# Query tokens in a fused ViT tower: five split float32r products per tile against two plain float32 products

## The chip, the cores and the metric

The kernel runs on one core of a Trainium2 chip. A time is the device time of one execution in microseconds (us), and the metric is the median over several executions. TensorE is called PE below, VectorE DVE, ScalarE ACT, GpSimd POOL and the DMA-issuing SyncE SP.

## What is computed

From images x (128 images, 12 channels, 224 x 224, float32), each 16 x 16 patch is summed per channel, which gives 196 tokens of 12 numbers, and each token is multiplied by a 12 x 192 matrix. Of the 196 tokens of an image the first 64 are queries and the other 132 are keys. After a layer norm the queries attend to the keys; the attention output goes through a projection, and the sum is `h`. Then comes the part that this change touches:

```
x2 = layernorm(h)                          # 192 channels
scores = sigmoid(x2 @ gate_weight.T)       # 8 experts; the best 2 are chosen through 4 groups
h1 = einsum('td,eid->tei', x2, w1)         # 8 experts, 128 inner channels
h3 = einsum('td,eid->tei', x2, w3)
y  = einsum('tei,edi,te->td', silu(h1) * h3, w2, cw)
z  = silu(x2 @ sw1.T) * (x2 @ sw3.T) @ sw2.T   # a shared ninth expert
out = h + y + z
```

All inputs and the output are float32. "First layer" means the products with w1, w3, sw1 and sw3; "router" means the product with gate_weight.

## The kernel before, in words

The 128 images are worked through in 8 groups of 16. A group has 2112 key tokens and 1024 query tokens, cut into 7 chunks: five of keys (384 to 512 tokens) and two of queries (512 each). For each chunk 9 experts are run, so a group has 63 steps: steps 0 to 44 are the key steps and steps 45 to 62 the query steps. PE's program is written out by hand (`ffn_pe`, L1527). In each step it issues the w1 product of the next step (`layer1`, k = 0), the w3 product of this step (k = 1), the second layer of the step two back (`layer2`, L1509), and then the items that a plan gives to this step (`AQ_PLAN`, `AK_PLAN`, L79 to L140): attention, transposes, router, sums. ACT makes silu of h1 (L913), POOL multiplies it with the routing weight that an SP-issued DMA has spread over the partitions (L752, L561), DVE multiplies that with h3 (L1266), and PE's second layer reads it. While one group runs, DVE and ACT sum the image tiles of later groups (L960, L801), and in the query steps DVE also computes the next group's key routing (`gates`, L1157).

A matmul contracts over partitions, of which there are 128, and there are 192 channels. For keys, the normalized token depends on 12 pooled numbers and a constant, so their first layer is one bf16 product of 126 rows (L1524). Queries have no such short form. Their normalized 192 channels are transposed in two parts, channels 0 to 127 and 128 to 191, by the item `XT` (L1451): four rounds a group, in steps 21, 22, 26 and 27. In an even round, four transposes fill a PSUM bank of 512 columns. In an odd round each tile's last 64 channels are written twice, by a transpose to partitions 0 to 63 and by a product with the identity to partitions 64 to 127 (L1460, L1461). ACT then copies the bank as float32r (L859) into `x0h` or `x1h`, the high part. DVE waits for that copy (`high_ready`) and subtracts it from the bank (L1152), which gives the low part `x0l` or `x1l`. The weights are split in the same way once, at the start (L1013 to L1019): `WT0h`, `WT0l`, and `WT1s`, which holds the high part of the last 64 channels in its first 64 partitions and the low part in the other 64. The router's weights `gT0h`, `gT0l`, `gT1s` likewise. With these, `layer1` makes a query product of 512 tokens as five float32r products (`products`, L1350 to L1354), added up in one PSUM bank: high x high, low weight x high, high weight x low for the 128 channels, then stacked weights x high and stacked weights x low for the 64. The router item `GQ` (L1462, step 28, two a group) does the same with 8 output rows.

The start of the kernel runs a list of rounds (`PREP`, L418) on PE with copies by DVE or ACT: transposing the weights (`W0`, `W1`), the router's (`gate`), and `Wc` (L1325), which multiplies the weights by the 12-row token matrix for the keys, in plain float32 and in three products: high, low and stacked. Between the rounds, DVE, ACT and POOL sum the first group's 21 image tiles. Only three tile buffers exist, so a tile's DMA waits until all of these engines have read the one three back.

Of the kernel before, what the change touches and what calls it, by code (L numbers as in the profile page):

```python
# [26 lines left out]
F32R = mybir.dt.float32r  # L27
# [115 lines left out]
DVE_KINDS = ("tok", "S", "H", "AH", "XT")  # L143
# [124 lines left out]
def build(nc, x, cw, proj_w, proj_b, gate_w, gate_b, w1, w2, w3, sw1, sw2, sw3, out):  # L268
    ctx = ExitStack()
    with ctx:  # L270
# [22 lines left out]
        WT0h = sb("WT0h", [128, 2 * EX * INTER], F32R)  # L293
        WT0l = sb("WT0l", [128, 2 * EX * INTER], F32R)
        WT1s = sb("WT1s", [128, 2 * EX * INTER], F32R)
        Wx = sb("Wx", [SPL * SPL * UC, 2 * EX * INTER + NE], BF16)
        W2T = sb("W2T", [INTER, EX, D])
        gT0h, gT0l, gT1s = sb("gT0h", [128, NE], F32R), sb("gT0l", [128, NE], F32R), sb("gT1s", [128, NE], F32R)
# [7 lines left out]
        x0h, x0l = sb("x0h", [128, 1024], F32R), sb("x0l", [128, 1024], F32R)  # L306
        x1h, x1l = sb("x1h", [128, 1024], F32R), sb("x1l", [128, 1024], F32R)
# [87 lines left out]
        high_ready = sem("high_ready")  # L395
# [63 lines left out]
        def split_dst(r):  # L459

            kind, i = PREP[r]
            if kind == "gate":
                return NE, (gT0h if i == 0 else gT1s)[:, :], gT0l[:, :] if i == 0 else None
            a, k = w4(i)
            a, n = a * 128, k * 128
            return n, (WT0h if kind == "W0" else WT1s)[:, a:a + n], WT0l[:, a:a + n] if kind == "W0" else None
# [312 lines left out]
        def _(act):  # L779
# [39 lines left out]
            def item(g, kind, i):  # L819
# [4 lines left out]
                if kind not in PE_KINDS or kind in DVE_KINDS and kind != "XT":  # L824
                    return
# [17 lines left out]
                elif kind == "X":  # L843
                    b0, nb = S_IMGS[i]
                    keys_out(X2T, ps[0:126, 0:nb * NK].rearrange("p (b t) -> p b t", b=nb), b0, nb).then_inc(aux_act, 1)
                elif kind == "ET":
                    if i == 0:

                        wait(act, cw_out[0], g.at(16, 16))
                        wait(act, cw_out[1], g.at(64, 64))  # L850
                    nc.scalar.copy(ET[:, 8 * (i % 2):8 * (i % 2) + 8, :].rearrange("p u q -> p (u q)"), ps[0:HT, :])\
                      .then_inc(aux_act, 1)
                elif kind == "M":
                    half, part = divmod(i, 2)
                    n = 2 * D if part == 0 else D
                    nc.scalar.copy(Msb[0:8 * CH, half, 2 * D * part:2 * D * part + n], ps[0:8 * CH, 0:n]).then_inc(aux_act, 1)
                elif kind == "XT":
                    q, part = divmod(i, 2)
                    nc.scalar.copy((x0h if part == 0 else x1h)[:, 512 * q:512 * q + 512], ps[:, :]).then_inc(high_ready, 1)  # L859
                elif kind == "GQ":  # L860
                    nc.scalar.copy(logT[:, 512 * i:512 * i + 512], ps[0:NE, :]).then_inc(aux_act, 1)
                elif kind in ("G", "GK"):
                    a, b = (0, 8) if kind == "G" else (8, GT)
                    nc.scalar.activation(gt[:, 0, NE * a:NE * b], ps[:, 0:NE * (b - a)], ACT.Exp, scale=-1.0)\
                      .then_inc(aux_act, 1)
                elif kind in ("CK", "CQ"):
                    n = 64 if (kind, i) == ("CK", 4) else 512
                    st = cw_stage[(kind, i)][:, 0:n]
                    nc.scalar.copy(st, ps[0:NE, 0:n]).then_inc(aux_act, 1)
                    at = 512 * i + (1024 if kind == "CK" else 0)  # L870
                    act.wait_ge(aux_act, g.at(BYACT[-1], BYACT[r]))
                    act.dma_start(cw_rows[g.par, :, at:at + n], st)\
                       .then_inc(cw_out[2 if kind == "CQ" else min(i, 1)], 16)
# [67 lines left out]
        def _(dve):  # L941
# [60 lines left out]
            def prep(r):  # L1002
# [10 lines left out]
                elif PREP[r][0] in ("W0", "W1", "gate"):  # L1013
                    n, high, low = split_dst(r)
                    ps = aux[r % 2]
                    plink(v.tensor_copy(high, ps[:, 0:n]))
                    if low is None:
                        high, low, ps = high[64:128], high[64:128], ps[64:128]
                    v.tensor_tensor(out=low, in0=ps[:, 0:n], in1=high.bitcast(F32), op=ALU.subtract).then_inc(prep_dve, 1)  # L1019
# [47 lines left out]
            def item(g, kind, i):  # L1067
# [80 lines left out]
                elif kind == "XT":  # L1148
                    q, part = divmod(i, 2)
                    high, low = (x0h, x0l) if part == 0 else (x1h, x1l)  # L1150
                    dve.wait_ge(high_ready, g.at(4, i + 1))
                    v.tensor_tensor(out=low[:, 512 * q:512 * q + 512], in0=ps[:, :],  # L1152
                                    in1=high[:, 512 * q:512 * q + 512].bitcast(F32), op=ALU.subtract).then_inc(aux_dve, 1)
                elif kind in ("gate_k", "gate_q"):
                    gates(g, i, *((8, GT, ("GK", 0)) if kind == "gate_k" else (0, 8, ("G", 0))))
# [128 lines left out]
        def _(pe):  # L1284
# [3 lines left out]
            for r, (kind, i) in enumerate(PREP):  # L1288
# [19 lines left out]
                elif kind == "gate":  # L1308
# [3 lines left out]
                    if i == 1:  # L1312
                        last = mm(ps[64:128, 0:NE], g_nat[:, 128:D], ident[0:NE, 0:NE], start=True, stop=True)
# [4 lines left out]
                elif kind == "W1":  # L1318

                    a, k = w4(i)  # L1320
                    for j in range(k):
                        nc.tensor.transpose(ps[0:64, 128 * j:128 * j + 128], w13_nat[:, a + j, 128:D], ident[:, :])
                        last = mm(ps[64:128, 128 * j:128 * j + 128], w13_nat[:, a + j, 128:D], ident[:, :],
                                  start=True, stop=True)
                elif kind == "Wc":  # L1325
# [3 lines left out]
                    for lo, hi, parts in ((0, m, [w[:, a:a + m] for w in (WT0h, WT0l, WT1s)]),  # L1329
                                          (m, n, [w[:, :] for w in (gT0h, gT0l, gT1s)])):  # L1330
                        if lo < hi:
                            for q in range(3):
                                last = mm(ps[0:CH, lo:hi], CWcT[q // 2], parts[q].bitcast(F32), start=(q == 0), stop=(q == 2))
# [15 lines left out]

            def products(o, left, right):  # L1350

                for q in range(len(left)):
                    ins = mm(o, left[q], right[q], start=(q == 0), stop=(q == len(left) - 1))  # L1353
                return ins  # L1354

            def item(g, kind, i):
# [94 lines left out]
                elif kind == "XT":  # L1451
# [3 lines left out]
                    for j in range(4):  # L1455
# [3 lines left out]
                        else:  # L1459
                            nc.tensor.transpose(ps[0:64, at], x2q[:, j, 128:D], ident[:, :])  # L1460
                            last = mm(ps[64:128, at], x2q[:, j, 128:D], ident[:, :], start=True, stop=True)  # L1461
                elif kind == "GQ":  # L1462

                    at = slice(512 * i, 512 * i + 512)
                    last = products(ps[0:NE, :], [gT0h[:, :], gT0l[:, :], gT0h[:, :], gT1s[:, :], gT1s[:, :]],
                                    [x0h[:, at], x0h[:, at], x0l[:, at], x1h[:, at], x1l[:, at]])
# [46 lines left out]
            def layer1(g, step, k):  # L1513
# [5 lines left out]
                if query:  # L1519
                    w, at = slice(w, w + INTER), slice(col, col + n)  # L1520
                    last = products(o[:, 0:n], [WT0h[:, w], WT0l[:, w], WT0h[:, w], WT1s[:, w], WT1s[:, w]],
                                    [x0h[:, at], x0h[:, at], x0l[:, at], x1h[:, at], x1l[:, at]])
# [60 lines left out]
```

## Time and profile before

| what | value |
|---|---|
| median of 3 runs | 1799.77 us (1799.73 to 1805.82) |
| the profiled execution's own time | 1794.41 us |
| its span, first to last instruction | 1792.6 us |
| mean granted TensorE clock | 0.950 of full speed |
| PE matmul busy | 84% of the span |
| DVE, ACT, POOL busy | 66%, 49%, 42% |
| HBM traffic | 242 GB/s over the span |

The profile records one execution. Its own time is 1.8 us above its span, and 5.4 us below the median of the runs. Busy time of PE is a union of matmuls whose ends are modelled, so the distance from one matmul's start to the next one's is the better measure of what a matmul costs while PE never waits.

### The profile page before, as it was taken

Reading aid. Unit: us, or ns where it says so; the run is one execution under the profiler, and the core shown is the slowest. Engines: PE = TensorE matmul, PEld = TensorE weight load, DVE = VectorE, ACT = ScalarE, POOL = GpSimd, SP = SyncE. Lnnn points to the kernel's source line nnn. Section 1 sums busy time; section 2 is a strip of 40 time slices with the busy share of each in tenths; the row PEclk is TensorE's granted clock in tenths of the full one; section 3 lists DMA queues with packets and bytes.
Section 4 is the critical chain, followed back from the end, with each engine's and each line's share of the span. In section 5 each row is a group of like instructions: output and inputs, shape, how many; then the busy total and the mean of one; then the engine's idle time right before and its main releaser. Section 6 shows DMA issues by size and latency. Waiting matters only on the chain. (4 is left out here: it accounts for less than half of the span.)

```text
span 1792.6 us, 29976 instructions
## 1 busy us (share of the span) xinstructions
PE 1509.6 (84%) x9094; PEld 1184.0 (66%) x9094; DVE 1178.3 (66%) x2060; ACT 879.1 (49%) x2809; POOL 761.5 (42%) x761
## 2 busy tenths in 40 slices
PE   1721698999899988989899988999899988999997
PEld 1201575877668765877668765777668765887686
DVE  5856686687768666667768676677768666355511
ACT  2333655556545645547535655546545644335310
POOL 4327244633373234623464243633373233733431
PEclk9955799999999989999999999999999989999998
DMA  9897777778677777777777687768777775223320
GB/s 341 358 361 276 300 276 272 276 276 291 245 280 260 281 262 268 273 275 274 256 247 297 241 292 278 276 253 299 256 263 280 268 262 158 70 64 111 96 84 24
DMA packets 127672, 440.11 MB, mean 246 GB/s; under 512 B 14221, under 2 KB 80930, under 8 KB 105998
## 3 DMA queue, kind: packets, MB, share of 16 engines
q1 hardware_dynamic: 126390, 436.79, 67.6%
q10 hardware_dynamic: 1112, 1.30, 0.3%
q8 instruction: 76, 1.25, 0.3%
q14 instruction: 94, 0.77, 0.1%
HBM read 413.86 MB, written 20.07 MB: 242 GB/s over the span
## 5 line engine op out<-in xcount | busy, mean ns | idle before, releaser
L752 POOL TENSOR_TENSOR ffn<-ffn 128x384 f32<-128x384 f32 (+2 forms) x448 | 510.3, 1144 | 888.7 <-ACT ffn L913 810.2
L1509 PE MATMUL bank<-W2T,ffn 128*128 128x192 f32 (+1 forms) x3600 | 705.7, 333 | 10.2 <-ACT stage L890 5.0
L1509 PEld LDWEIGHTS bank<-W2T,ffn 128*128 128x128 f32 (+1 forms) x3600 | 604.9, 191 | 79.8 <-issue 16.5
L1266 DVE TENSOR_TENSOR ffn<-bank,ffn 128x384 f32<-128x384 f32 (+2 forms) x504 | 310.4, 617 | 349.3 <-PE bank L1353 151.8
L960 DVE TENSOR_REDUCE pooled<-xt 128x3 f32<-128x768 f32 (+2 forms) x375 | 447.8, 1195 | 18.5 <-DMA xt<-in_x 17.9
L913 ACT ACTIVATE ffn<-bank 128x384 f32<-128x384 f32 (+2 forms) x504 | 272.3, 542 | 370.3 <-PE bank L1524 141.3
L801 ACT ACTIVATE xt<-xt 128x256 f32<-128x256 f32 x809 | 329.7, 414 | 83.7 <-DMA xt<-in_x 76.1
L1524 PE MATMUL bank<-X2T,Wx 126*128 126x384 bf16 (+2 forms) x720 | 202.6, 355 | 46.7 <-DVE ffn L1266 31.9
L801 ACT ACTIVATION_READ_ACCUMULATOR xt<-xt 128x1 f32 x809 | 158.6, 196 | 0.0
L1353 PE MATMUL bank<-x0h,WT0h 128*128 128x512 f32 x288 | 130.5, 453 | 6.0 <-DVE ffn L1266 6.0
L1524 PEld LDWEIGHTS bank<-X2T,Wx 126*128 126x128 bf16 x720 | 58.2, 100 | 103.7 <-DVE ffn L1266 46.1
L1353 PE MATMUL bank<-x1l,WT1s 128*128 128x512 f32 x288 | 113.9, 395 | 0.0
L1353 PE MATMUL bank<-x1h,WT1s 128*128 128x512 f32 x288 | 113.8, 395 | 0.0
L1353 PE MATMUL bank<-x0l,WT0h 128*128 128x512 f32 x288 | 113.6, 395 | 0.0
L1353 PE MATMUL bank<-x0h,WT0l 128*128 128x512 f32 x288 | 113.6, 394 | 0.0
L707 POOL TENSOR_TENSOR stat<-stat,mhalf 98x16 f32<-98x16 f32 x32 | 94.8, 2970 | 21.9 <-DVE stat L1085 13.6
L1353 PEld LDWEIGHTS bank<-x0h,WT0h 128*128 128x128 f32 x288 | 54.3, 189 | 24.6 <-DVE ffn L1266 9.0
L1353 PEld LDWEIGHTS bank<-x1l,WT1s 128*128 128x128 f32 x288 | 54.0, 188 | 13.1
L1353 PEld LDWEIGHTS bank<-x0l,WT0h 128*128 128x128 f32 x288 | 54.0, 188 | 13.0
L1353 PEld LDWEIGHTS bank<-x1h,WT1s 128*128 128x128 f32 x288 | 54.0, 188 | 13.0
L1353 PEld LDWEIGHTS bank<-x0h,WT0l 128*128 128x128 f32 x288 | 54.4, 189 | 5.9
L841 ACT CAST UTq<-bank 126x128 bf16<-126x128 f32 x64 | 17.0, 265 | 84.0 <-PE bank L1433 84.0
(234 smaller groups left out, 1786.1 us busy)
## 6 DMA issues: line engine op xcount, KB each, us to landing
xt<-in_x SPq DMA_DIRECT2D x168, 1792.0 KB, 8.2
ffn<-cw_rows SPq DMA_DIRECT2D x192, 256.0 KB, 6.8
ffn<-cw_rows SPq DMA_DIRECT2D x192, 192.0 KB, 8.8
out<-stage SPq DMA_DIRECT2D x192, 96.0 KB
ffn<-cw_rows SPq DMA_DIRECT2D x64, 224.0 KB, 7.1
h2q<-Msb SPq DMA_DIRECT2D x64, 54.0 KB
ffn<-in_L_ffn_w SPq DMA_DIRECT2D x2, 768.0 KB
attw<-in_L_ffn_w SPq DMA_DIRECT2D x1, 512.0 KB
```

Source lines behind the costliest of these rows:

```text
L707: nc.gpsimd.tensor_tensor(out=stat[:, 3 * a + 1, u], in0=stat[:, 3 * a, u], in1=mhalf[0:HT, u], op=ALU.pow).then_inc(rstd_ready, 1)
L752: nc.gpsimd.tensor_tensor(out=cwb[slot][:, 0:n], in0=silu[(g.par + step) % 2][:, 0:n], in1=cwb[slot][:, 0:n], op=ALU.mult).then_inc(scaled, 1)
L801: last = nc.scalar.activation(src[:, :, j, :], src[:, :, j, :], ACT.Copy, accum_out=pooled[:, t // HALF, at:at + 1])
L841: nc.scalar.copy(UTq[:, :].rearrange("p (b t) -> p b t", b=GB)[:, 2 * i:2 * i + 2, :], src[:, :, 0:NQ])
L913: nc.scalar.activation(silu[(g.par + step) % 2][:, 0:n], h_ps(g, step, 0)[:, 0:n], ACT.Silu)\
L960: ins = v.tensor_reduce(out=pooled[:, t // HALF, at + lo:at + hi], in_=src[:, lo:hi, :, :], axis=AX.XY, op=ALU.add)
L1266: v.tensor_tensor(out=h[step % HR][:, 0:n], in0=h_ps(g, step, 1)[:, 0:n], in1=(silu[p] if e == NE else cwb[(c * NE + e) % CW_RING])[:, 0:n ...
L1353: ins = mm(o, left[q], right[q], start=(q == 0), stop=(q == len(left) - 1))
L1509: last = mm(o, h[step % HR][:, 128 * t:128 * t + m], W2T[:, e, :], start=(e == 0 and t % 2 == 0), stop=(e == NE), skip_group_check=True)
L1524: last = mm(o[:, 0:n], Wx[:, w:w + INTER], X2T[:, col:col + n], start=True, stop=True)
```

## The change

The float32r type is gone, and with it all low parts. `x0` and `x1` hold the transposed tokens in float32 (128 and 64 partitions), `WT0` and `WT1` the first-layer weights, `gT0` and `gT1` the router's. Each query product is made of two float32 products, one over 128 rows and one over 64. `XT` becomes a round that ACT alone empties: it leaves the list of DVE's kinds and no longer has the second write of the 64 channels. In the start, a weight round is one DVE copy, without a subtraction, `W1` has one transpose a tile, and `Wc` has two products in place of three. The semaphore `high_ready` is gone.

```diff
-DVE_KINDS = ("tok", "S", "H", "AH", "XT")
+DVE_KINDS = ("tok", "S", "H", "AH")
...
-        WT0h = sb("WT0h", [128, 2 * EX * INTER], F32R)
-        WT0l = sb("WT0l", [128, 2 * EX * INTER], F32R)
-        WT1s = sb("WT1s", [128, 2 * EX * INTER], F32R)
+        WT0, WT1 = sb("WT0", [128, 2 * EX * INTER]), sb("WT1", [D - 128, 2 * EX * INTER])
...
-        x0h, x0l = sb("x0h", [128, 1024], F32R), sb("x0l", [128, 1024], F32R)
-        x1h, x1l = sb("x1h", [128, 1024], F32R), sb("x1l", [128, 1024], F32R)
+        x0, x1 = sb("x0", [128, 1024]), sb("x1", [D - 128, 1024])
...
                 elif kind == "XT":
                     q, part = divmod(i, 2)
-                    nc.scalar.copy((x0h if part == 0 else x1h)[:, 512 * q:512 * q + 512], ps[:, :]).then_inc(high_ready, 1)
+                    x, n = (x0, 128) if part == 0 else (x1, D - 128)
+                    nc.scalar.copy(x[:, 512 * q:512 * q + 512], ps[0:n, :]).then_inc(aux_act, 1)
...
                 elif PREP[r][0] in ("W0", "W1", "gate"):
-                    n, high, low = split_dst(r)
-                    ps = aux[r % 2]
-                    plink(v.tensor_copy(high, ps[:, 0:n]))
-                    if low is None:
-                        high, low, ps = high[64:128], high[64:128], ps[64:128]
-                    v.tensor_tensor(out=low, in0=ps[:, 0:n], in1=high.bitcast(F32), op=ALU.subtract).then_inc(prep_dve, 1)
+                    v.tensor_copy(*transposed(r)).then_inc(prep_dve, 1)
...
-                elif kind == "XT":
-                    q, part = divmod(i, 2)
-                    high, low = (x0h, x0l) if part == 0 else (x1h, x1l)
-                    dve.wait_ge(high_ready, g.at(4, i + 1))
-                    v.tensor_tensor(out=low[:, 512 * q:512 * q + 512], in0=ps[:, :],
-                                    in1=high[:, 512 * q:512 * q + 512].bitcast(F32), op=ALU.subtract).then_inc(aux_dve, 1)
...
                         else:
-                            nc.tensor.transpose(ps[0:64, at], x2q[:, j, 128:D], ident[:, :])
-                            last = mm(ps[64:128, at], x2q[:, j, 128:D], ident[:, :], start=True, stop=True)
+                            last = nc.tensor.transpose(ps[0:64, at], x2q[:, j, 128:D], ident[:, :])
                 elif kind == "GQ":
 
                     at = slice(512 * i, 512 * i + 512)
-                    last = products(ps[0:NE, :], [gT0h[:, :], gT0l[:, :], gT0h[:, :], gT1s[:, :], gT1s[:, :]],
-                                    [x0h[:, at], x0h[:, at], x0l[:, at], x1h[:, at], x1l[:, at]])
+                    mm(ps[0:NE, :], gT0[:, :], x0[:, at], start=True, stop=False)
+                    last = mm(ps[0:NE, :], gT1[:, :], x1[:, at], start=False, stop=True)
...
                 if query:
                     w, at = slice(w, w + INTER), slice(col, col + n)
-                    last = products(o[:, 0:n], [WT0h[:, w], WT0l[:, w], WT0h[:, w], WT1s[:, w], WT1s[:, w]],
-                                    [x0h[:, at], x0h[:, at], x0l[:, at], x1h[:, at], x1l[:, at]])
+                    mm(o[:, 0:n], WT0[:, w], x0[:, at], start=True, stop=False)
+                    last = mm(o[:, 0:n], WT1[:, w], x1[:, at], start=False, stop=True)
```

## Rows read from the trace of the kernel before

**Rows 1.** The page: busy time of each engine over the span.

```profile
PE 1509.6 (84%) x9094; PEld 1184.0 (66%) x9094; DVE 1178.3 (66%) x2060; ACT 879.1 (49%) x2809; POOL 761.5 (42%) x761
```

**Rows 2.** Windows by stage: stretch, length, busy of each engine, PEclk, DMA share, GB/s.

```profile
320.00:391.60 71.60, 69.95 (x400) 59.12 (x399) 51.65 (x73) 39.76 (x147) 34.49 (x30) 1.00 0.69 254
391.60:517.90 126.30, 109.95 (x722) 84.43 (x722) 91.18 (x180) 70.54 (x211) 52.41 (x45) 0.99 0.80 288
...
589.40:722.90 133.50, 114.11 (x723) 87.51 (x722) 91.08 (x181) 70.75 (x211) 52.55 (x45) 0.95 0.77 273
...
1711.50:1777.20 65.70, 65.70 (x325) 55.92 (x324) 13.35 (x20) 11.07 (x20) 20.22 (x16) 1.00 0.16 48
```

**Rows 3.** Timeline of PE, one query step: start, us, operation, shapes, count.

```profile
354.67 0.53 PE L1353 MATMUL bank<-x0h,WT0h 128*128 128x512 f32 x1
355.03 0.39 PE L1353 MATMUL bank<-x0h,WT0l 128*128 128x512 f32 x1
...
357.13 1.46 PE L1509 MATMUL bank<-W2T,ffn 128*128 128x192 f32 x8
358.30 0.53 PE L1353 MATMUL bank<-x0h,WT0h 128*128 128x512 f32 x1
```

**Rows 4.** Timeline of PE in the start, plain float32 products of `Wc`.

```profile
67.43 1.02 PE L1333 MATMUL bank<-WT0h,rq 128*12 128x512 f32 x2
...
74.30 1.02 PE L1333 MATMUL bank<-WT1s,gs 128*12 128x512 f32 x2
```

**Rows 5.** Groups of PE instructions, shapes apart: busy, mean ns | idle before.

```profile
L1509 PE MATMUL bank<-W2T,ffn 128*128 128x192 f32 x3456 | 671.7, 332 | 10.2 <-ACT stage L890 5.0 <-DVE stage L1247 4.4
L1353 PE MATMUL bank<-x0h,WT0h 128*128 128x512 f32 x288 | 130.5, 453 | 6.0 <-DVE ffn L1266 6.0
L1458 PE MATMUL bank<-ident,attw 128*128 128x128 f32 x64 | 10.0, 279 | 16.6 <-DVE attw L1146 9.3 <-issue 7.3
```

**Rows 6.** The same view of weight loads.

```profile
L1509 PEld LDWEIGHTS bank<-W2T,ffn 128*128 128x128 f32 x3456 | 590.9, 193 | 65.4 <-ACT stage L890 13.3 <-DVE stage L1247 7.0 <-issue 2.1
```

**Rows 7.** Timeline of PE around steps 21 and 22, the first two `XT` rounds.

```profile
451.56 0.63 PE L1458 MATMUL bank<-ident,attw 128*128 128x128 f32 x4 [1.09 <-DVE attw L1146]
452.02 0.25 PE L1449 MATMUL bank<-CWx,UTq 126*128 126x192 bf16 x1
...
454.19 0.27 PE L1460 MATMUL bank<-ident,attw 128*64 128x128 f32 x1
454.39 0.43 PE L1461 MATMUL bank<-ident,attw 128*64 128x128 f32 x2
...
456.54 0.26 PE L1449 MATMUL bank<-CWx,UTq 126*128 126x192 bf16 x1
```

**Rows 8.** Who uses `x1l` (ns min/median/max, first and last start), and DVE's wait there.

```profile
L1152 DVE TENSOR_TENSOR x1l<-bank,x1h x16: 691/692/692, 259.4 to 1675.0; 128x512 fp32r<-128x512 f32 x16
...
ACT x1h L859: 34.0, 16
```

**Rows 9.** The longest of PE's waits in 320 to 391.6: total, times, longest.

```profile
PE bank L1353 <- DVE ffn L1266: 0.8, 1, 0.8
```

**Rows 10.** Timelines of PE and POOL at the start of the next group.

```profile
397.88 0.68 PE L1402 MATMUL bank<-ident,attw 64*128 64x64 f32 x8 [1.87 <-DVE attw L1105]
...
394.77 2.91 POOL L752 TENSOR_TENSOR ffn<-ffn 128x384 f32<-128x384 f32 x3 [8.40 <-DMA ffn<-cw_rows]
```

**Rows 11.** Groups of DVE instructions in 0 to 192: busy, mean ns | idle before.

```profile
L1019 DVE TENSOR_TENSOR WT0l<-bank,WT0h 128x512 fp32r<-128x512 f32 x4 | 2.8, 692 | 0.1
```

**Rows 12.** Windows of the start, columns as in rows 2.

```profile
60.00:72.00 12.00, 10.93 (x24) 2.65 (x24) 8.84 (x15) 5.20 (x24) 4.62 (x10) 1.00 1.01 430
72.00:80.00 8.00, 4.36 (x13) 1.03 (x12) 7.75 (x10) 2.66 (x12) 3.40 (x7) 1.00 0.51 183
```

**Rows 13.** Timeline of PE, a product with 64 rows and the one after.

```profile
424.15 0.56 PE L1426 MATMUL bank<-projT,Asb 64*96 64x192 f32 x2
424.64 0.50 PE L1524 MATMUL bank<-X2T,Wx 126*128 126x384 bf16 x2
```

More of the change, by code:

```diff
@@ L26 @@
 BF16 = mybir.dt.bfloat16
-F32R = mybir.dt.float32r
 ACT = mybir.ActivationFunctionType
@@ L291, in build @@
         projT = sb("projT", [NQ, 3, D])
-        WT0h = sb("WT0h", [128, 2 * EX * INTER], F32R)
-        WT0l = sb("WT0l", [128, 2 * EX * INTER], F32R)
-        WT1s = sb("WT1s", [128, 2 * EX * INTER], F32R)
+        WT0, WT1 = sb("WT0", [128, 2 * EX * INTER]), sb("WT1", [D - 128, 2 * EX * INTER])
         Wx = sb("Wx", [SPL * SPL * UC, 2 * EX * INTER + NE], BF16)
         W2T = sb("W2T", [INTER, EX, D])
-        gT0h, gT0l, gT1s = sb("gT0h", [128, NE], F32R), sb("gT0l", [128, NE], F32R), sb("gT1s", [128, NE], F32R)
+        gT0, gT1 = sb("gT0", [128, NE]), sb("gT1", [D - 128, NE])
         gbias = sb("gbias", [128, NE])
@@ L457, in prep_copies, with transposed @@
             raise AssertionError(kind)
-        def split_dst(r):
+        def transposed(r):
             kind, i = PREP[r]
+            ps = aux[r % 2]
             if kind == "gate":
-                return NE, (gT0h if i == 0 else gT1s)[:, :], gT0l[:, :] if i == 0 else None
+                return (gT0[:, :], ps[:, 0:NE]) if i == 0 else (gT1[:, :], ps[0:64, 0:NE])
             a, k = w4(i)
             a, n = a * 128, k * 128
-            return n, (WT0h if kind == "W0" else WT1s)[:, a:a + n], WT0l[:, a:a + n] if kind == "W0" else None
+            return (WT0[:, a:a + n], ps[:, 0:n]) if kind == "W0" else (WT1[:, a:a + n], ps[0:64, 0:n])
         block = ctx.enter_context(nc.Block())
@@ L823, in item @@
                     return
-                if kind not in PE_KINDS or kind in DVE_KINDS and kind != "XT":
+                if kind not in PE_KINDS or kind in DVE_KINDS:
                     return
@@ L1311, in _ @@
                     last = nc.tensor.transpose(ps[0:n, 0:NE], g_nat[:, 128 * i:128 * i + n], ident[0:NE, 0:NE])
-                    if i == 1:
-                        last = mm(ps[64:128, 0:NE], g_nat[:, 128:D], ident[0:NE, 0:NE], start=True, stop=True)
                 elif kind == "W0":
@@ L1321, in _ @@
                     for j in range(k):
-                        nc.tensor.transpose(ps[0:64, 128 * j:128 * j + 128], w13_nat[:, a + j, 128:D], ident[:, :])
-                        last = mm(ps[64:128, 128 * j:128 * j + 128], w13_nat[:, a + j, 128:D], ident[:, :],
-                                  start=True, stop=True)
+                        last = nc.tensor.transpose(ps[0:64, 128 * j:128 * j + 128], w13_nat[:, a + j, 128:D], ident[:, :])
                 elif kind == "Wc":
@@ L1328, in _ @@
                     m = min(n, WCOLS - a)
-                    for lo, hi, parts in ((0, m, [w[:, a:a + m] for w in (WT0h, WT0l, WT1s)]),
-                                          (m, n, [w[:, :] for w in (gT0h, gT0l, gT1s)])):
+                    for lo, hi, parts in ((0, m, [w[:, a:a + m] for w in (WT0, WT1)]),
+                                          (m, n, [w[:, :] for w in (gT0, gT1)])):
                         if lo < hi:
-                            for q in range(3):
-                                last = mm(ps[0:CH, lo:hi], CWcT[q // 2], parts[q].bitcast(F32), start=(q == 0), stop=(q == 2))
+                            mm(ps[0:CH, lo:hi], CWcT[0], parts[0], start=True, stop=False)
+                            last = mm(ps[0:CH, lo:hi], CWcT[1][0:D - 128], parts[1], start=False, stop=True)
                 elif kind == "w2":
@@ L1347, in _ @@
             pe.wait_ge(ready, 1)
[L1350 to L1354, printed above, removed]
             def item(g, kind, i):
```

1 line of the change is left out of this document (removed).

## The prediction

> **What bounds the kernel now.** I read the page first: PE is the busiest engine, DVE far behind [rows 1]. An average over stages hides what matters, so I cut the span at the ends of the 45th and 63rd DVE product (L1266) of a group, which separates key and query steps, and asked for windows. In a query stage PE is busy 69.95 of 71.60 us at full clock while DVE is busy 51.65. In the last group, where nothing is left to prepare, DVE falls to 13.35 us and PE is busy for all 65.70 us [rows 2]. PE's longest wait in a query stage is 0.8 us [rows 9], and its gaps there sum to under 2 us [rows 2]. So the query steps are bound by PE, and whatever PE gains or loses there is the kernel's. Key stages are mixed: PE is busy 109.95 of 126.30 us and waits for the rest [rows 2]; a saving there returns only in part.
>
> Next I read PE's timeline inside one query step, by starts and not by durations, because durations overlap. Ten float32r products of 512 columns start between 354.67 and the next operation's start at 357.13. From the second start on, nine take 2.10 us, so one costs 0.233 us, and the first exposes another 0.13 us of weight load. The step repeats after 3.63 us [rows 3].
>
> The price of a plain float32 product of 512 columns stands in the same trace, in the start, where `Wc` reads the split weights as float32. Each product is recorded as two instructions ("x2"), and from 67.43 to 74.30 eight products take 6.87 us: 0.859 us each [rows 4], at full clock [rows 12]. The second layer agrees on the doubling: 3456 instructions for 1728 products [rows 5].
>
> **The change, part by part.**
>
> *Query first layer.* 288 product groups, two to a step, so 144 steps [rows 5]. Removed: 10 x 0.233 = 2.33 us. Added: 4 x 0.859 = 3.44 us. Net +1.10 us a step, x 144 = **+158.7 us**, all on PE, which is the bound. Bounds of the new price: the start's products load 12 weight columns and these 128. The nearest row with 128 weight columns is the second layer, eight instructions of 192 columns from 357.13 to 358.30, plus the 0.13 us by which the next first start overlaps: 0.162 us each, 0.325 a product, 0.867 us if scaled to 512 columns [rows 3]. That gives +1.13 a step (+163). If the weight load exposed at the head vanished too, +0.98 a step (+141). Its weight load takes 193 ns [rows 6] and stays under an instruction of 0.43 us.
>
> *Router.* two groups of five a group of images, 16 in all, become groups of two: eight times 1.10 = **+8.8 us** in step 28; bounds 7.8 and 9.1.
>
> *XT on PE.* An odd round takes 2.35 us (454.19 to 456.54), since each tile changes between a transpose and a two-instruction product; the even round, four transposes, 0.46 us (451.56 to 452.02) [rows 7]. The new odd round is four transposes too. 16 odd rounds save 16 x 1.89 = **-30 us** at most. This is a key stage, but PE does not wait between these steps. On DVE the subtraction goes, 32 of 0.69 us, and its 34.0 us of waiting for ACT's high copy in odd rounds [rows 8]. DVE's later items come sooner, x2 among them, for which PE's even rounds wait 9.3 us in all [rows 5]. ACT still has a copy a round, and frees the bank. If DVE's tile sums or POOL's chain then end these steps, half is lost: bounds -15 and -42. I take -30, since both engines become shorter.
>
> *Idle that longer query steps cover.* At the start of a group POOL waits 8.40 us for the routing weights' DMA, and PE then 1.87 us [rows 10]; within the query stage under 2 us [rows 2]. Each of the last steps gives that DMA 1.1 us more. Over seven boundaries, bounds 0 and 7 x 3.5 = -25; I take **-8**, because SP issues these loads behind others that are themselves tied to steps.
>
> *Start.* Four subtractions of 0.69 us for `WT0l` [rows 11], as many for `WT1s` and smaller ones leave DVE (about 7 us), and five of PE's 0.86 us products leave `Wc` [rows 4]. Up to 72 us the tile DMAs run at 430 GB/s, so nothing is to be had; in 72 to 80 DVE is busy 7.75 us of 8 and DMA falls to 0.51 of its share [rows 12]. Only those 4 us can come back, or 8 if DVE sets more of it: bounds 0 and -8, I take **-3**.
>
> *Clock.* Two key stages with the same work took 126.3 us at a granted 0.99 and 133.5 at 0.95 [rows 2]. A shorter odd round changes PE's pauses there, in either sense: 0, with +-10. Query stages already have 1.00.
>
> Sum: 158.7 + 8.8 - 30 - 8 - 3 = **+126.5 us**, from 1792.6 to a span of 1919, some 1921 for that execution. The median of the runs shown stands 5.4 us above the profiled execution, so 1799.8 + 126.5 = **1926 us**.
>
> **Rivals.**
>
> *Half-rate float32 (faster).* Suppose a float32 product with 128 weight columns takes one pass at half rate, 0.43 us, not two instructions of that. A step then changes by 4 x 0.43 - 2.33 = -0.61 us, -93 for 152 such groups of ten, and with the other terms the kernel comes to about 1799.8 - 93 - 41 = 1666. It decides if a product costs under 2.33/4 = 0.58 us. Against it stand two rows: "x2" on each start product, and 3456 instructions for W2T [rows 4, 5]. For it speaks only that no row shows 128 weight columns with 512 moving. The Trainium skill, Perfetto Trace Analysis, section Engine Utilization, puts the tensor core's rate at "÷2 for FP32_LOW_HIGH", which would be this rival if one product were one such instruction. By this case's row, it describes each half. The skill's FP8 and Floating Point Precision, TensorE Precision Notes, gives "True FP32: 4 passes", which the 0.859 us agree with.
>
> *The 64-row product rides along (faster).* If it ran beside its neighbour, a step would have two paid products: 1.72 - 2.33 = -0.61, again about 1666. Against: a 64-row product of 192 columns takes 0.49 us with its change to the next operation, no less than the 0.325 of 128 rows [rows 13, 3]. The skill, TensorE: Matmul & The Clock Gate, Part 3, lets small products run together if they use distinct row groups; the neighbours here have 128 rows.
>
> *Weight loads exposed.* If each of the eight float32 loads of a step cost half its 193 ns in the open, +0.77 a step, +117: about 2043. Against: in the second layer, 193 ns loads stand behind starts 0.162 apart [rows 3, 6].
>
> *Given back.* If key stages return more than I allow, or a fifth of the query steps hide it, +40 to +85: about 1865.
>
> *No effect.* The products still run as float32r: only XT and the start gain, 1799.8 - 41 = 1759. The start's rows, where a float32 view costs 0.859, are against it.
>
> **How the numbers follow.** Chances: main 0.88, given back 0.04, half rate 0.03, riding along 0.02, exposed loads 0.02, no effect 0.01. About 0.5% (9 us) is what a measurement of this kernel can tell from no change. Faster: 0.03 + 0.02 + 0.01 = 0.06; same 0.01, for a return larger still; slower 0.93. The low ends together give 141 + 8 - 42 - 25 - 8 - 10 = +64, the high ends 163 + 9 - 15 + 10 = +167. All ends at once are unlikely; I leave out the outer quarter on the low side and keep the high: 1885 to 1960.
>
> **What would show it.** L1353 gone; in its place at layer1 1152 float32 instructions of 512 columns, starts 0.43 us apart, and 64 for the router. The query stage in the middle groups at 71.5 + 18 x 1.10 = 91 us, PE still full, DVE's share lower, and the last group's at 85. Odd XT rounds under 0.6 us and no DVE row for XT. Key stages 2 to 4 us shorter. Starts 0.2 us apart, or a query stage under 75 us, would break the main case; a query stage right and key stages unchanged would put the time near 1950.

## The result, and the profile after

The changed kernel takes 1995.88 us (median of 4 runs, 1991.09 to 1999.54), the kernel before 1799.75 us: a ratio of 1.1116, 95% interval 1.1078 to 1.1155. The direction was forecast, the size was not: +196 us in place of +126.5, outside the range. The quotient of these two medians is 1.1090, a little below the ratio. Later executions of the kernel before have medians of 1791 to 1794 us, and differences called "by the ratios" below are differences of ratios times some 1795 us. The profiled execution took 1996.78 us, with a span of 1995.0 us.

The engines' line on the page of the changed kernel, and its most costly PE groups with the shapes kept apart ("PEld" is a weight load):

```profile
PE 1740.2 (87%) x8612; PEld 1063.5 (53%) x8612; DVE 1131.8 (57%) x2016; ACT 885.5 (44%) x2809; POOL 759.5 (38%) x761
```

```profile
L1484 PE MATMUL bank<-W2T,ffn 128*128 128x192 f32 x3456 | 685.3, 336 | 7.0 <-ACT stage L887 6.2
L1497 PE MATMUL bank<-x,WT 64*128 64x512 f32 x576 | 323.2, 641 | 0.0
L1496 PE MATMUL bank<-x,WT 128*128 128x512 f32 x576 | 315.6, 630 | 0.0
```

There are the 1152 float32 instructions of the first layer that were forecast, two for each product; L1496 is the product of 128 rows and L1497 the one of 64. Every other engine is less busy than in [rows 1], as a share.

The same windows as in [rows 2], cut at the same DVE products (L1252 in this kernel): a query stage, the key stage after it, and the last group's query stage.

```profile
539.00:641.00 102.00, 101.77 (x365) 47.74 (x365) 49.87 (x73) 40.82 (x147) 34.94 (x31) 1.00 0.58 205
641.00:765.90 124.90, 110.28 (x702) 83.17 (x700) 88.74 (x176) 70.69 (x211) 51.58 (x44) 0.97 0.76 270
...
1881.10:1979.50 98.40, 98.40 (x289) 43.74 (x288) 13.37 (x20) 11.05 (x20) 19.93 (x16) 1.00 0.11 32
```

A query stage grew from 71.5 to 102.0 us, where 91 were forecast, and PE still has no gaps in it. So the bound was right, and the price of a product was wrong. The timeline of PE in one step of the changed kernel shows it:

```profile
366.41 1.02 PE L1496 MATMUL bank<-x,WT 128*128 128x512 f32 x2
367.37 1.12 PE L1497 MATMUL bank<-x,WT 64*128 64x512 f32 x2
368.42 1.13 PE L1496 MATMUL bank<-x,WT 128*128 128x512 f32 x2
369.47 1.12 PE L1497 MATMUL bank<-x,WT 64*128 64x512 f32 x2
370.53 1.57 PE L1484 MATMUL bank<-W2T,ffn 128*128 128x192 f32 x8
371.93 0.59 PE L1496 MATMUL bank<-x,WT 128*128 128x512 f32 x1
```

From one product's start to the next it is 1.05 us, not 0.86 as in [rows 4]. The weight loads of the same stretch (a row merges several loads, in brackets the idle time of the load path):

```profile
366.25 0.35 PEld L1496 LDWEIGHTS bank<-x,WT 128*128 128x128 f32 x2
367.36 0.29 PEld L1497 LDWEIGHTS bank<-x,WT 64*128 64x128 f32 x2 [0.76 <-issue]
368.42 0.30 PEld L1496 LDWEIGHTS bank<-x,WT 128*128 128x128 f32 x2 [0.76 <-issue]
369.47 0.29 PEld L1497 LDWEIGHTS bank<-x,WT 64*128 64x128 f32 x2 [0.76 <-issue]
370.52 1.27 PEld L1484 LDWEIGHTS bank<-W2T,ffn 128*128 128x128 f32 x8 [0.76 <-issue]
```

From 367.36 on, each product's first load begins together with the product (368.42 and 368.42). The product at 366.41 is different: it has 128 rows and follows 128 rows, and its first load, at 366.25, stands ahead of it. In the kernel before, loads stand one product ahead. These are two rows of its load timeline; PE starts the second product (`x0h` by `WT0l`) at 355.03 and the third (`x0l` by `WT0h`) at 355.27:

```profile
355.04 0.19 PEld L1353 LDWEIGHTS bank<-x0l,WT0h 128*128 128x128 f32 x1
355.27 0.19 PEld L1353 LDWEIGHTS bank<-x1h,WT1s 128*128 128x128 f32 x1
```

The load for the product that starts at 355.27 already begins at 355.04. After the change nothing is loaded ahead where 128 and 64 rows meet. This is the rival of exposed loads in its effect. Its mechanism, though, was given as any load of a float32 product. The start's products of [rows 4] differ from these in two ways: they load 12 weight columns and not 128, and every neighbour there has 128 rows, where here 128 and 64 alternate. Such a change of the row count between neighbours is called a switch below. The experiments tell the two apart.

### The profile page after: what moved, and what is told of

Its sections match the earlier page's. It is cut to its first block, busy times and chain, and to the rows that moved or that the text cites. A ratio compares the mean times of both kernels' runs of the same rounds, so it can differ in the third digit from the quotient of the medians.

```text
span 1995.0 us, 28922 instructions
## 1 busy us (share of the span) xinstructions
PE 1740.2 (87%) x8612; PEld 1063.5 (53%) x8612; DVE 1131.8 (57%) x2016; ACT 885.5 (44%) x2809; POOL 759.5 (38%) x761
## 4 chain that ended last, share of the span: by engine, by line
PE 70%; issue 8%; DVE 7%; DMA 6%; POOL 3%; ACT 2%; SPq 2%; ACTq 0%; DVEq 0%; POOLq 0%
PE bank L1484 24%; PE bank L1497 15%; PE bank L1496 14%; PE bank L1499 4%; DMA xt<-in_x 3%; DVE pooled L957 2%; DMA ffn<-cw_rows 2%; POOL ffn L748 2%; PE bank L1384 1%; DVE ffn L1252 1%; PE bank L1366 1%; SPq L528 1%; PE bank L1383 1%; PE bank L1397 1%; PE bank L1457 1%
## 5 line engine op out<-in xcount | busy, mean ns | idle before, releaser
L1484 PE MATMUL bank<-W2T,ffn 128*128 128x192 f32 (+1 forms) x3600 | 719.2, 337 | 7.0 <-ACT stage L887 6.2
L1252 DVE TENSOR_TENSOR ffn<-bank,ffn 128x384 f32<-128x384 f32 (+2 forms) x504 | 310.3, 618 | 620.2 <-PE bank L1497 412.2
L1497 PE MATMUL bank<-x,WT 64*128 64x512 f32 x576 | 323.2, 641 | 0.0
L1496 PE MATMUL bank<-x,WT 128*128 128x512 f32 x576 | 315.6, 630 | 0.0
L1499 PE MATMUL bank<-X2T,Wx 126*128 126x384 bf16 (+2 forms) x720 | 201.1, 353 | 42.0 <-DVE ffn L1252 29.1
L1497 PEld LDWEIGHTS bank<-x,WT 64*128 64x128 f32 x576 | 84.8, 184 | 218.4 <-issue 218.4
L1496 PEld LDWEIGHTS bank<-x,WT 128*128 128x128 f32 x576 | 88.8, 189 | 112.8 <-issue 98.7
L874 ACT CAST X2T<-bank 126x384 bf16<-126x384 f32 (+1 forms) x48 | 20.7, 449 | 83.0 <-PE bank L1419 82.8
L1457 PE MATMUL bank<-ident,gt 128*8 128x128 f32 x200 | 28.7, 284 | 23.9 <-DVE gt L1212 22.4
L659 POOL TENSOR_TENSOR ffn<-xt 128x256 f32<-128x256 f32 x31 | 22.9, 739 | 68.1 <-DMA xt<-in_x 67.8
L887 ACT COPY stage<-bank 128x384 f32<-128x384 f32 x80 | 29.2, 418 | 40.3 <-PE bank L1484 40.1
L1419 PE MATMUL bank<-identb,SPT 98*126 98x34 bf16 (+1 forms) x256 | 20.4, 224 | 28.1 <-DVE SPT L1056 28.1
```

The lines of the kernel that those rows point to most:

```text
L887: ins = nc.scalar.copy(st[:, 2 * D * b:2 * D * b + full], out_ps[b][:, 0:full])
L1252: v.tensor_tensor(out=h[step % HR][:, 0:n], in0=h_ps(g, step, 1)[:, 0:n], in1=(silu[p] if e == NE else cwb[(c * NE + e) % CW_RING])[:, 0:n ...
L1457: last = nc.tensor.transpose(ps[0:NE, 128 * j:128 * j + 128], gt[:, 0, at:at + NE], ident[:, :])
L1484: last = mm(o, h[step % HR][:, 128 * t:128 * t + m], W2T[:, e, :], start=(e == 0 and t % 2 == 0), stop=(e == NE), skip_group_check=True)
L1496: mm(o[:, 0:n], WT0[:, w], x0[:, at], start=True, stop=False)
L1497: last = mm(o[:, 0:n], WT1[:, w], x1[:, at], start=False, stop=True)
```

## The experiments

**1. The 64-row product padded to 128 rows.** `WT1`, `gT1` and `x1` get 128 partitions; the lower halves are zeros, written once.

```diff
-        x0, x1 = sb("x0", [128, 1024]), sb("x1", [D - 128, 1024])
+        x0, x1 = sb("x0", [128, 1024]), sb("x1", [128, 1024])
...
+            for pad in (WT1, gT1, x1):
+                link(nc.gpsimd.memset(pad[64:128, :], 0.0))
```

> The changed kernel with the 64-row product padded by zeros to 128 rows; same number of products, columns and weight loads. Switch theory: what made the float32 products dearer than forecast (1.05 us instead of 0.86) is the switch between a product of 128 rows and one of 64, four a query step, some 0.2 us each (the next weight load starts 0.09 us after the columns have passed, and 0.107 us of it is in the open). Without switches a product costs 0.86 us, a query stage falls from 102 to about 87 us, and the kernel to 1996 - 119 = about 1877 us. Wide-load theory: a float32 product of 512 columns with a 128-column weight load always pays for its first load, whatever its rows: 1996 us, starts still 1.05 us apart per product.

Measured: 1881.98 us, ratio to the kernel before 1.0492 (1.0438 to 1.0545), so 112 us less than the change by the ratios, where the theory of the switch gave 1877 us. PE's timeline:

```profile
366.59 1.02 PE L1499 MATMUL bank<-x,WT 128*128 128x512 f32 x2
367.45 1.02 PE L1498 MATMUL bank<-x,WT 128*128 128x512 f32 x2
368.31 1.02 PE L1499 MATMUL bank<-x,WT 128*128 128x512 f32 x2
369.17 1.46 PE L1486 MATMUL bank<-W2T,ffn 128*128 128x192 f32 x8
```

A product costs 0.86 us again, with twice the rows. The wide-load theory, that 512 columns with 128 weight columns always pay for their first load, falls. A query stage takes 88.3 us:

```profile
526.70:615.00 88.30, 88.07 (x366) 53.41 (x365) 52.80 (x72) 40.69 (x147) 35.05 (x31) 1.00 0.62 224
```

**2. The same products in another order.** Nothing padded; the w3 group takes its 64-row product first.

```diff
-                    mm(o[:, 0:n], WT0[:, w], x0[:, at], start=True, stop=False)
-                    last = mm(o[:, 0:n], WT1[:, w], x1[:, at], start=False, stop=True)
+                    parts = [(WT0, x0), (WT1, x1)] if k == 0 else [(WT1, x1), (WT0, x0)]
+                    mm(o[:, 0:n], parts[0][0][:, w], parts[0][1][:, at], start=True, stop=False)
+                    last = mm(o[:, 0:n], parts[1][0][:, w], parts[1][1][:, at], start=False, stop=True)
```

> The changed kernel with the order of the two products turned round in the w3 group only, so that the two 64-row products of a step stand side by side: 128, 64, 64, 128 rows. No product, load or byte is added or removed; the changes of row count fall from four to two a step. Switch theory: 144 x 2 x 0.2 = 58 us less, about 1938 us, and no gap between the two 64-row products. Wide-load theory: each product still pays for its first load, 1996 us.

Measured: 1940.88 us, ratio 1.0843 (1.0782 to 1.0904), 49 us (by the ratios) below the change, where 58 were expected. The two switches that went are worth 0.17 us each over 144 steps. This is the cleanest of the runs, since it moves instructions and adds or removes none:

```profile
366.70 1.02 PE L1497 MATMUL bank<-x,WT 128*128 128x512 f32 x2
367.65 1.12 PE L1498 MATMUL bank<-x,WT 64*128 64x512 f32 x2
368.62 1.02 PE L1497 MATMUL bank<-x,WT 64*128 64x512 f32 x2
369.56 1.13 PE L1498 MATMUL bank<-x,WT 128*128 128x512 f32 x2
370.53 1.46 PE L1484 MATMUL bank<-W2T,ffn 128*128 128x192 f32 x8
```

A switch shows in two halves. About 0.1 us is lost before it (0.95 for the 128-row product ahead of one) and about 0.1 after it (0.97 for the first 64-row product, 1.12 in place of 1.02 as its duration).

**3. Padded to 72 rows.** The padding of experiment 1 with 72 in place of 128, shown against experiment 1.

```diff
-                link(nc.gpsimd.memset(pad[64:128, :], 0.0))
+                link(nc.gpsimd.memset(pad[64:72, :], 0.0))
```

> As the padding to 128 rows, but only to 72. Switch theory with its border at 64 rows (in the kernel before, a 72-row product stands between 126-row ones without a gap): same as padding to 128, about 1877 us. If the border lay at each 32 rows, or any difference of rows counted: 1996 us. Wide-load theory: 1996 us.

Measured: 1880.52 us, ratio 1.0506 (1.0449 to 1.0563), the same as 128 rows within the intervals.

```profile
366.74 1.02 PE L1498 MATMUL bank<-x,WT 128*128 128x512 f32 x2
367.60 1.02 PE L1499 MATMUL bank<-x,WT 72*128 72x512 f32 x2
368.46 1.46 PE L1486 MATMUL bank<-W2T,ffn 128*128 128x192 f32 x8
```

So it is neither a difference of rows as such nor a border at each 32 rows: 72 and 128 are alike to PE, and 64 is not. The Trainium skill, TensorEngine Tiling (Array Packing), section Tiling Modes, lists row tilings of one tile of 128 rows, two of 64 or four of 32, and says that "Changing tiling mode (not just tile) drains the TensorE". It gives no time for it, and it does not say that an ordinary product of 64 rows amid others runs in another mode; that is a reading of these runs. All three agree with it: some 0.19 us a switch for these products, drain and late load together. No run shows the mode itself.

**4. The switch in float32r.** The kernel before, its fourth and fifth product cut to 64 rows. This leaves out the low part of the last 64 channels' weights.

```diff
-                    last = products(o[:, 0:n], [WT0h[:, w], WT0l[:, w], WT0h[:, w], WT1s[:, w], WT1s[:, w]],
-                                    [x0h[:, at], x0h[:, at], x0l[:, at], x1h[:, at], x1l[:, at]])
+                    last = products(o[:, 0:n], [WT0h[:, w], WT0l[:, w], WT0h[:, w], WT1s[0:64, w], WT1s[0:64, w]],
+                                    [x0h[:, at], x0h[:, at], x0l[:, at], x1h[0:64, at], x1l[0:64, at]])
```

> The kernel before with its fourth and fifth float32r product of each first-layer group cut from 128 rows to 64 (the low parts of the last 64 channels' weights are left out). Same five one-pass products, half the rows in two of them, two switches a group added. Switch theory, if it holds for float32r too: 0.1 to 0.2 us a switch, 4 a query step less the 0.13 us that a step's first load exposes now, so query stages of 80 to 85 us in place of 71.5 and a kernel of about 1870 to 1900 us. If only two-instruction float32 products pay: 1794 us, and fewer rows never cost anything.

Measured: 1867.21 us, ratio 1.0414 (1.0375 to 1.0452): 74 us slower by the ratios for multiplying fewer rows, and just under the 1870 to 1900 us that were expected. One group of five:

```profile
367.08 0.50 PE L1353 MATMUL bank<-x0h,WT0h 128*128 128x512 f32 x1
367.42 0.39 PE L1353 MATMUL bank<-x0h,WT0l 128*128 128x512 f32 x1
367.65 0.40 PE L1353 MATMUL bank<-x0l,WT0h 128*128 128x512 f32 x1
367.98 0.49 PE L1353 MATMUL bank<-x1h,WT1s 64*128 64x512 f32 x1
368.31 0.39 PE L1353 MATMUL bank<-x1l,WT1s 64*128 64x512 f32 x1
368.64 1.57 PE L1509 MATMUL bank<-W2T,ffn 128*128 128x192 f32 x8
```

Starts at a switch are 0.33 to 0.34 us apart instead of 0.23, before it and after it. The cost belongs to the switch and not to the plain float32 type. A query stage took 82.6 us instead of 71.5.

**5. The transpose rounds alone, DVE kept.** In the kernel before, DVE writes the last 64 channels twice, side by side, and an odd round is four transposes of 128 columns.

```diff
-                        v.tensor_scalar(x2q[:, t % 4, :], h2q[:, t, :], bst[:, t, 6:7], rq[:, 1, t:t + 1],
+                        v.tensor_scalar(x2q[:, t % 4, 0:D], h2q[:, t, :], bst[:, t, 6:7], rq[:, 1, t:t + 1],
+                                        ALU.subtract, ALU.mult)
+                        v.tensor_scalar(x2q[:, t % 4, D:256], h2q[:, t, 128:D], bst[:, t, 6:7], rq[:, 1, t:t + 1],
                                         ALU.subtract, ALU.mult).then_inc(x2_ready, 1)
...
-                            nc.tensor.transpose(ps[0:64, at], x2q[:, j, 128:D], ident[:, :])
-                            last = mm(ps[64:128, at], x2q[:, j, 128:D], ident[:, :], start=True, stop=True)
+                            last = nc.tensor.transpose(ps[:, at], x2q[:, j, 128:256], ident[:, :])
```

> The kernel before (five float32r products, DVE's subtraction and its wait kept), with one part changed alone: DVE writes the last 64 channels of the normalized tokens twice, side by side, and an odd transpose round becomes four transposes of 128 columns instead of four transposes and four two-instruction products with the identity. PE saves 16 x 1.89 = 30 us in the key steps; DVE gets 64 short operations more. If all of PE's saving reaches the end: 1800 - 30 = 1770 us. If DVE's chain ends those steps and half is lost: 1785 us. If it is hidden: 1800 us.

Measured: 1794.13 us against 1794.37, ratio 1.0006 (0.9979 to 1.0033): the same. The profiled execution was the fastest of its ten, at 1785.53 us. In it the ten steps 20 to 29 of the third group took 27.5 us in place of 29.1. The first row is of the kernel before, the other two are the third and the second group of this run, and the last is PE's row for the even rounds, which has 16.6 us of idle time in [rows 5]:

```profile
651.20:680.30 29.10, 26.65 (x153) 20.09 (x154) 23.25 (x50) 14.36 (x46) 11.36 (x11) 1.00 0.75 258
...
650.30:677.80 27.50, 22.99 (x137) 18.68 (x138) 24.84 (x58) 14.34 (x45) 11.32 (x10) 1.00 0.79 276
450.30:479.00 28.70, 24.41 (x137) 20.03 (x138) 24.89 (x57) 14.27 (x44) 11.36 (x10) 0.94 0.74 266
...
L1460 PE MATMUL bank<-ident,attw 128*128 128x128 f32 x64 | 10.4, 288 | 32.6 <-DVE attw L1148 17.3 <-issue 15.3
```

PE's saving of 3.7 us a group (26.65 to 22.99) goes two ways. Half becomes waiting: the even rounds wait for DVE's normalized tokens, which now take 64 more writes and which PE now reaches earlier, and PE's idle time before them grows from 16.6 to 32.6 us in the whole kernel. Then the clock: in the kernel before, all eight groups run these steps at full clock, and here three do not (0.94, 0.94 and 0.89, with 28.7 to 30.4 us). In the second group PE stood idle for 2.05 us up to 456.14, where it had been 1.09 before, and from 457 to 460 the granted clock is 0.50, the lower of its two levels. All ten executions have a mean clock of 0.938 to 0.944, the 13 of the kernel before 0.945 to 0.954. Together the ten steps of the eight groups still lose 7 us. That the median lost nothing is not accounted for further.

**6. The transpose rounds without DVE's subtraction.** Experiment 5, and DVE's subtraction and its wait go too. This leaves out the low parts of the tokens. It is not quite what the change does, as the text below says: DVE's second write of the 64 channels is in this run and not in the changed kernel, whose odd rounds transpose 64 columns into 64 partitions.

```diff
-                    v.tensor_tensor(out=low[:, 512 * q:512 * q + 512], in0=ps[:, :],
-                                    in1=high[:, 512 * q:512 * q + 512].bitcast(F32), op=ALU.subtract).then_inc(aux_dve, 1)
...
+            for low in (x0l, x1l):
+                link(nc.gpsimd.memset(low[:, :].bitcast(F32), 0.0))
```

> The wide transposes, and also DVE's subtraction and its wait for ACT's copy taken away (the low parts of the tokens are left out: they are zeros, written once, so five products still run). This is what the change does in the transpose rounds, without its products. Theory: PE's saving of 1.89 us a round reaches the end only when DVE no longer stands in those rounds; steps 19 to 29 then take 25.3 us instead of 29.1, some 27 to 30 us less than before, 1765 us. If the clock or another engine takes it back: 1785 to 1794 us.

Measured: 1779.21 us, ratio 0.9940 (0.9911 to 0.9968), 11 us less by the ratios where 27 to 30 were expected. The same ten steps took 26.8 us, 2.3 less than before and not the 3.7 that PE saved. The rows are these ten steps here and in the changed kernel, and PE's even rounds here and in the changed kernel:

```profile
650.60:677.40 26.80, 22.99 (x137) 18.72 (x138) 22.80 (x54) 14.36 (x45) 11.39 (x10) 1.00 0.82 293
697.20:723.80 26.60, 24.41 (x135) 18.23 (x136) 21.02 (x46) 14.43 (x45) 11.41 (x11) 1.00 0.82 295
...
L1456 PE MATMUL bank<-ident,attw 128*128 128x128 f32 x64 | 10.1, 280 | 28.7 <-DVE attw L1150 14.8 <-issue 13.9
L1434 PE MATMUL bank<-ident,attw 128*128 128x128 f32 x64 | 10.0, 279 | 13.8 <-DVE attw L1138 7.4 <-issue 6.4
```

PE's waits took up the rest, and the rows say which. PE's idle time before the even rounds is 28.7 us here, 12 more than the 16.6 before, and 13.8 in the changed kernel. The 64 second writes cost DVE 27.9 us in this run, and they are the writes for which PE waits (L1150). So the run gives less than the change's rounds would by themselves, by some 12 us as an estimate from these two rows. No run has the narrow rounds with the five products.

**7. The change without its transpose rounds and start.** The kernel before, with only the products replaced. This leaves out the low parts, which are still made.

```diff
-                    last = products(ps[0:NE, :], [gT0h[:, :], gT0l[:, :], gT0h[:, :], gT1s[:, :], gT1s[:, :]],
-                                    [x0h[:, at], x0h[:, at], x0l[:, at], x1h[:, at], x1l[:, at]])
+                    last = products(ps[0:NE, :], [gT0h[:, :].bitcast(F32), gT1s[0:64, :].bitcast(F32)],
+                                    [x0h[:, at].bitcast(F32), x1h[0:64, at].bitcast(F32)])
...
-                    last = products(o[:, 0:n], [WT0h[:, w], WT0l[:, w], WT0h[:, w], WT1s[:, w], WT1s[:, w]],
-                                    [x0h[:, at], x0h[:, at], x0l[:, at], x1h[:, at], x1l[:, at]])
+                    last = products(o[:, 0:n], [WT0h[:, w].bitcast(F32), WT1s[0:64, w].bitcast(F32)],
+                                    [x0h[:, at].bitcast(F32), x1h[0:64, at].bitcast(F32)])
```

> The kernel before with one part of the change alone: first layer and router take two plain float32 products (128 and 64 rows) of the high parts, the low parts are still made but not read (left out of the sums). Start, transpose rounds and DVE's subtractions as before. Theory: query stages as in the changed kernel (102 us, +245 us in all), the router's +12, and the idle at a group's start covered (-25): 1794 + 232 = about 2025 us, 30 us above the changed kernel, which is what its transpose rounds and start give. If those parts give nothing: 1996 us.

Measured: 2034.77 us, ratio 1.1347 (1.1317 to 1.1377), which is 41 us above the change by the ratios, where 30 were expected. Its query stages take 102 us as well. The ten steps of the third group:

```profile
708.30:739.00 30.70, 28.24 (x151) 19.60 (x152) 23.26 (x50) 14.43 (x45) 11.39 (x10) 1.00 0.74 259
```

So the transposes and the start do give some 41 us back inside the change. Over the eight groups the ten steps take 232 us in the kernel before, 243 here, with the router's dearer products, and 211 in the changed kernel: the narrow transpose rounds are worth 32 us.

**8. The wait at a group's start.** After the change, the third group's first DVE product ends 1.6 us after the last one of the group before it, instead of 5.5. To see whether that wait could be had without slower query steps, the kernel before does its key routing a step earlier.

```diff
-    AK_PLAN.setdefault(53 + _n // 5, []).append(("gate_k", _n))
+    AK_PLAN.setdefault(53 + _n // 6, []).append(("gate_k", _n))
...
-                if step >= 61 and left:
-                    for ahead in ((0, 1) if step == 61 else (2, 3, 4)):
+                if step >= 60 and left:
+                    for ahead in ((0, 1), (2, 3, 4), ())[step - 60]:
```

> The kernel before with the next group's key routing done one step earlier (six DVE routing operations a step instead of five, the transposes and row stores in steps 58 and 59, the row loads issued in steps 60 and 61). Nothing is added or removed. If the 40 us that the key stages lost with the change are in part the wait of POOL for the routing rows at a group's start (5.0 to 5.9 us from one group's last product to the next group's first, 1.6 us after the change), this wait goes here too: up to 7 x 3.5 = 25 us less, 1770 us. If those steps are held by something else, or if the denser routing operations delay DVE: 1794 us.

Measured: 1807.26 us, ratio 1.0074 (1.0048 to 1.0099): 0.7% slower, where no time or 25 us less were expected. Windows of the border and the nineteen steps after it in the kernel before, then of the query stage, the border and these steps in this run:

```profile
589.40:594.90 5.50, 4.49 (x32) 4.06 (x30) 1.67 (x4) 1.65 (x4) 1.70 (x2) 1.00 0.85 249
594.90:651.20 56.30, 48.80 (x364) 39.36 (x364) 36.80 (x68) 33.90 (x101) 17.92 (x18) 0.91 0.78 283
...
522.20:595.30 73.10, 70.02 (x399) 59.05 (x398) 52.57 (x73) 39.97 (x147) 34.90 (x31) 1.00 0.66 239
595.30:596.90 1.60, 1.60 (x12) 1.47 (x11) 1.60 (x4) 0.49 (x1) 0.55 (x2) 1.00 1.02 426
596.90:655.60 58.70, 51.83 (x386) 42.05 (x384) 36.72 (x69) 35.02 (x103) 18.29 (x18) 0.91 0.80 295
```

The wait did go, from 5.5 to 1.6 us. It came back as 1.6 us in the query stage and in the steps behind it: 58.7 us where the kernel before has 56.3. Over the eight groups of the two profiles the borders fall from 36 to 15 us, the query stages grow from 565 to 574, and the nineteen steps behind a group's first from 418 to 440. In these steps the granted clock is 0.91 in four groups here and in two before, and such groups take 56 to 59 us, those at full clock 49 to 50. Why the clock falls in more groups is not shown. Earlier routing rows, then, are not worth what they free. In the float32r run of experiment 4, whose query stages are longer too, the border is 2.2 us, so longer query steps cover this wait whatever lengthens them.

**9. Both of the last ideas together.** Wide transposes with the earlier routing rows.

> The wide transposes and the earlier routing rows together, five float32r products kept. If each gives its part: about 10 us (the wide transposes in the profile) and up to 25 us, so 1760 to 1770 us. If the earlier rows give nothing: 1794 us.

Measured: 1807.02 us, ratio 1.0088 (1.0053 to 1.0122), where 1760 to 1770 us or no change were expected. Here too nothing of the freed time arrives. The six executions have a mean clock of 0.931 to 0.938.

**10. A version from what was learnt.** The wide transposes, and the key steps' own 64-row product (`M`) padded to 72 rows.

```diff
-        Asb = sb("Asb", [NQ, 2, 8 * CH])
+        Asb = sb("Asb", [72, 2, 8 * CH])
...
+            for pad in (Asb, projT):
+                link(nc.gpsimd.memset(pad[64:72, :, :], 0.0))
```

> The wide transposes, and the projection product M, the key steps' own 64-row product, padded by zeros from 64 to 72 rows. Switch theory: two switches fewer at each of four M items a group, 0.1 to 0.2 us each, 3 to 10 us of PE time in all, in stages where PE also waits for others: 1785 to 1794 us, faster than before by 5 us at most. If the key stages' waits take it all: the same as before.

Measured: 1787.58 us against 1793.01, ratio 0.9977 (0.9957 to 0.9996). By the ratio it is 4 us faster than the kernel before, within the 5 us that were expected. Its interval ends just below no change and overlaps that of experiment 5, so what the padding adds to the wide transposes is not shown. Of the versions that leave nothing out it has the lowest ratio.

## Why the prediction was wrong

By its own steps, against the two profiled spans (+202.4 us):

- *PE bounds the query steps*: right. 99.8% busy in 102.0 us, 98.40 of 98.40 in the last group.
- *Query first layer, +158.7 us*: **the step that failed.** Measured +247 us (the eight query stages sum to 812 us instead of 565). The failed term is the price of a float32 product: 0.859 us was taken from products whose neighbours all had 128 rows. Between 128 and 64 rows it is 1.053 us. The sentence that its weight load "stays under an instruction of 0.43 us" does not hold there: the load starts with its own product (368.42). Experiment 1, which only takes the switches away, has query stages of 703 us in all, 109 less; 4 switches x 144 steps x 0.194 us are 112. Without switches the term is 138 us, near its lower bound of 141: the first load of a step stands ahead of its product (366.25 and 366.41), and the 0.13 us head in [rows 3] goes.
- The row that would have told it was shown. In [rows 13] the 64-row product takes 0.49 us to the next operation where 128 rows take 0.325. The prediction read this as "no less", against the rival that it rides along, and did not ask what the other 0.165 us were. The bounds for an unseen 64-row product should have come from it.
- *Exposed loads*, the rival at 2% with 2043 us, had the nearest size and the wrong ground. It was dismissed by [rows 3, 6], where no row count changes.
- *Router, +8.8 us*: +11, from (4 x 0.954 - 2.45) x 8, where 0.954 is the mean distance of its four products (491.82 to 495.64) and 2.45 its ten float32r products (472.16 to 474.61 in the timeline). It has the same switches with 8 weight columns, at 0.095 us each. Experiment 7 agrees: with the router changed and the transposes not, the ten steps of the eight groups grow by 12 us.
- *XT, -30 us*: these ten steps went from 29.1 to 26.6 us with the router's 1.4 us in them, so -3.9 us a group, some -31 in all, and 32 between experiment 7 and the changed kernel: right, and with its reason, "both engines become shorter". Experiments 5 and 6 returned 0 and 11 us, but both make DVE write 64 channels twice, which the change does not, and PE waits for it.
- *Idle covered, -8 us*: -21, near its bound. The border fell from 5.0 to 7.6 us to 1.6 to 4.7 over six groups, and POOL's waiting for the routing weights' DMA (`cw_rows`) from 70.2 to 3.3 us in the whole kernel. So the reason for taking only 8, that SP issues these loads behind others, held back less than was assumed.
- *Start, -3 us*: the first DVE product came 3.0 us earlier. Right.
- *Clock, 0 +- 10 us*: query stages stayed at 1.00, and the mean granted clock of the key stages rose a little, from 0.969 to 0.975. Its share of the time is not separated from the other terms.
- *The range*: the high ends add up to 1799.8 + 167 = 1967 us, and not to the 1960 that was given for keeping them. With the switches, 1996 us lies outside either. No sum leads to the +40 to +85 us of "given back".

Together: 247 + 11 - 31 - 21 - 3 = 203 us, of the 202.4 measured.

## What to carry to other kernels

Count the changes of a matmul's row count across 64, not only columns and passes: in a dense stream each cost 0.1 to 0.2 us here, and eight rows of zeros, or another order of the same products, took it away. When the price of an operation is taken from a row, look at what stands before and after it in that row, and when a row of the very shape shows more than the formula, the surplus is the finding. When one part of a change is tried alone, compare the rows that wait for it with those of the whole change: here 64 short DVE writes that only the trial had hid some 12 of 30 us in PE's waits.

## What the runs showed of the hardware that was not expected

- A product of 64 rows between products of 128 is dearer than one padded to 128: 1.05 against 0.86 us in float32, with starts 0.33 against 0.23 us apart in float32r. A product of 72 rows is like one of 128.
- The cost of a switch was larger with more weights to load: 0.194 us with 128 float32 weight columns, 0.095 with 8.
- Cutting two of five products to half their rows slowed the kernel by 4.1%.
- Taking work from PE can cost clock. With less work in the ten steps and longer pauses before the even rounds, the granted clock fell to 0.94 or 0.89 in three of eight groups (experiment 5), where it was 1.00 in all before.
